# Second norm and router inside the attention across the batch, and modulation rows in the first layer's block

## What is computed

```python
mod = (silu(c) @ wmod).reshape(8, 6, 1, 256)
sa, ca, ga, sb, cb, gb = (mod[:, i] for i in range(6))
ga = (2 * (ga >= 0) - 1) * maximum(abs(ga), 0.25)      # gb likewise
x = x + ga * attention(layernorm(x) * (1 + ca) + sa)
x = x + gb * ffn(layernorm(x) * (1 + cb) + sb)
```

```python
h1 = hidden + attention_across_batch(layernorm(hidden) * w1 + b1)
tokens = layernorm(h1) * w2 + b2                       # the second norm
probs = softmax(tokens @ router_weight)                # 8 experts, top 2, capacity 1280
out = h1 + moe(tokens, probs)
```

## Time and profile before

| | us |
|---|---|
| median of 3 runs | 3240.66 |
| lowest, highest | 3238.57, 3241.61 |
| the profiled execution, its time | 3246.79 |
| the profiled execution, its span | 3245.0 |
| TensorE busy | 2931.1 (90%) |
| VectorE busy | 1657.6 (51%) |
| ScalarE busy | 1369.5 (42%) |
| GpSimd busy | 856.0 (26%) |
| mean granted TensorE clock | 0.944 |

### The profile page before, as it was taken

One profiled execution on the slowest core, in us unless ns is written; L12 is line 12 of the kernel. 1 busy time (PEld: TensorE's weight loads), 2 busy tenths in 40 slices (PEclk: granted clock), 3 DMA queues, 4 the chain that ended last, 5 costly groups with the idle time before them and its releaser, 6 DMA issues. The chain is left out here.

```text
span 3245.0 us, 52986 instructions
## 1 busy us (share of the span) xinstructions
PE 2931.1 (90%) x20772; PEld 1994.1 (61%) x20772; DVE 1657.6 (51%) x5057; ACT 1369.5 (42%) x2997; POOL 856.0 (26%) x830
## 2 busy tenths in 40 slices
PE   5889899975999999999999999999999688879993
PEld 2566666653575757666666666666565343668882
DVE  2566777644555544444444444455554576541114
ACT  2666666632444444445454535353433211112222
POOL 1001111122333332322323233233332100115554
PEclk8999999997999999999999999999999898669996
DMA  4110011004000000000000000100000000202325
GB/s 134 18 18 18 18 18 18 14 3 160 8 4 9 6 17 28 1 1 1 16 29 1 1 1 12 32 6 6 11 6 6 10 1 1 91 24 79 73 85 176
DMA packets 65135, 93.94 MB, mean 29 GB/s; under 512 B 9931, under 2 KB 52942, under 8 KB 63848
## 3 DMA queue, kind: packets, MB, share of 16 engines
q1 hardware_dynamic: 57208, 74.24, 7.9%
q0 software_dynamic: 7680, 16.32, 2.0%
HBM read 59.31 MB, written 27.36 MB: 27 GB/s over the span
## 5 line engine op out<-in xcount | busy, mean ns | idle before, releaser
L1371 PE MATMUL bank<-h2T,w 128*128 128x512 f32 x1024 | 479.4, 606 | 5.1 <-ACT gT L1309 3.7
L1409 PE MATMUL bank<-w,gT 128*128 128x256 f32 x2048 | 465.9, 381 | 0.0
L1409 PEld LDWEIGHTS bank<-w,gT 128*128 128x128 f32 x2048 | 379.3, 190 | 49.7 <-issue 0.5
L1046 POOL TENSOR_TENSOR prob<-prob,rsum 128x512 f32<-128x512 f32 (+1 forms) x256 | 238.1, 951 | 589.9 <-DVE rsum L1193 589.9
L1371 PEld LDWEIGHTS bank<-h2T,w 128*128 128x128 f32 x1024 | 182.4, 190 | 224.1 <-issue 173.9
L1309 ACT ACTIVATE gT<-bank,vec 128x512 f32<-128x512 f32 x256 | 175.1, 687 | 286.0 <-PE bank L1371 284.6
L633 ACT ACTIVATE y<-y,least 128x128 f32<-128x128 f32 (+3 forms) x512 | 251.9, 554 | 50.3 <-DVE least L520 50.2
L520 DVE CUSTOM_DVE_ANT_0 y<-bank,mask 128x128 f32<-128x128 f32 (+3 forms) x512 | 223.9, 486 | 77.0 <-PE bank L726 75.5
L1199 DVE COPY probT<-bank 128x1024 f32<-128x1024 f32 (+1 forms) x128 | 139.2, 1087 | 227.4 <-PE bank L1425 227.4
L1170 DVE CUSTOM_DVE_ANT_0 prob<-bank,mask 128x256 f32<-128x256 f32 (+1 forms) x512 | 164.3, 387 | 167.3 <-PE bank L1361 167.3
L1281 ACT ACTIVATE prob<-prob,least 128x256 f32<-128x256 f32 (+1 forms) x512 | 239.6, 471 | 15.8 <-DVE least L1170 15.4
(11 more groups left out here) (291 smaller groups left out, 5074.9 us busy)
## 6 DMA issues: line engine op xcount, KB each, us to landing
w<-in_W SPq DMA_DIRECT2D x8, 1024.0 KB, 5.5
expert_parts<-zeros SPq DMA_DIRECT2D x8, 1024.0 KB, 16.0
we<-in_we SPq DMA_DIRECT2D x16, 512.0 KB
rows<-modulation SPq DMA_DIRECT2D x40, 128.0 KB, 3.0
x<-in_x SPq DMA_DIRECT2D x8, 512.0 KB, 9.8
prob<-score SPq DMA_DIRECT2D x64, 64.0 KB, 2.4
probT<-score SPq DMA_DIRECT2D x64, 64.0 KB, 2.4
y<-expert_parts SPq DMA_DIRECT2D x8, 512.0 KB, 8.8
```

The lines of the kernel that those rows point to most:

```text
L1046: nc.gpsimd.tensor_tensor(two, two, rsum[:, at:at + 2].unsqueeze(2).to_broadcast([P, 2, width]), ALU.mult).then_inc(s["probs"], 1)
L1371: ins = nc.tensor.matmul(M[m % 2][:, :], w1[:, k, m * P:(m + 1) * P], h2T[:, k, :], start=(k == 0), stop=(k == KD - 1))
L1409: ins = nc.tensor.matmul(M[i][:, (t % 2) * D:(t % 2 + 1) * D], gT[:, m, t * P:(t + 1) * P], w2[:, m, :], start=(m == 0), stop=(m == MF - 1))
```

## The change

Two parts, independent of each other.

**The opening goes into the first layer's block.** `opening` is gone. The modulation becomes seven more pieces of the first layer's list: `("MOD", (l, m), 0)`, block m of layer l, and `("MT", i, 0)`, the turning of sa, ca (i = 0) or sb, cb (i = 1). `MOD (0, 0)` and `MT 0` stand first in `OPEN0`; the others go into parts 1 and 3 of slots 0 to 2. SyncE's order of loads is new: both cT, block (0, 0) of the weights, x of batch 0, the three projection matrices, x of batch 1, the other five blocks of weights; then `fixed` and the placements of batch 0; then x of batches 2 to 7, wo, the three ffn matrices and mu. Each has its own semaphore or count, and each user waits for its own. The six stores of the rows stand ahead of SyncE's part of slot 4, the wait for them ahead of slot 5. The weights and rows of the modulation lie in buffers that the layer uses later; `fixed` moves from y to probT. GpSimd makes the identity in place and its masks in another order.

```diff
+MODULATION = {(0, 1): [("MOD", (0, 1), 0)], (0, 3): [("MOD", (0, 2), 0)], (1, 1): [("MT", 1, 0)],
+              (1, 3): [("MOD", (1, 0), 0)], (2, 1): [("MOD", (1, 1), 0)], (2, 3): [("MOD", (1, 2), 0)]}
...
-OPEN0 = [("L", 0, 0), ("L", 1, 0), ("Q", 0, 0), ("Q", 1, 0), ("K", 0, 0), ("K", 1, 0), ("V", 0, 0), ("V", 1, 0),
+OPEN0 = [("MOD", (0, 0), 0), ("MT", 0, 0), ("L", 0, 0), ("L", 1, 0), ("Q", 0, 0), ("Q", 1, 0), ("K", 0, 0), ("K", 1, 0), ("V", 0, 0), ("V", 1, 0),
...
+                if n == QUADS:
+                    sp.wait_ge(s["mod_ready"], 6)
+                    for l in range(2):
+                        for m in range(3):
+                            sp.dma_start(c.mod_dram[l, :, m * T:(m + 1) * T], rows[l][m]).then_inc(s["store"], 16)
+                if n == QUADS + 1:
+                    sp.wait_ge(s["store"], 6 * 16)
...
+            def modulation(x):
+                _, (l, m), _ = x
+                full(dve, x)
+                block = rows[l][m]
+                emptied(nc.vector.tensor_copy(block, bank_of(x)[0:B, :]), x)
+                drained(dve, x)
+                if m == 0:
+                    v = block[:, D:2 * D]
+                    nc.vector.tensor_scalar(v, v, 1.0, None, ALU.add).then_inc(s["mod_ready"], 1)
+                    return
+                if m == 2:
+                    v = block[:, 0:D]
+                    nc.vector.tensor_scalar(v, v, 1.0, None, ALU.add)
+                v = block[:, 0:D] if m == 1 else block[:, D:2 * D]
+                steps(nc.vector.tensor_scalar(sign, v, 0.0, 2.0, ALU.is_ge, ALU.mult))
...
             stats(0)
+            taken(OPEN0[0:1])
             norm(0, None)
+            taken(OPEN0[1:2])
             stats(1)
...
+                    if kind == "MOD":
+                        l, m = i
+                        if l == 0 and m < 2:
+                            pe.wait_ge(s[("cond_loaded", "wm_loaded")[m]], (3, 5)[m] * 16)
+                        for k in range(KD):
+                            ins = nc.tensor.matmul(bank[0:B, :], cT[:, l, k, :], wm[l][m][:, k, :], start=(k == 0),
+                                                   stop=(k == KD - 1))
...
                         if i == 0 and kind == "Q":
-                            pe.wait_ge(s["load"], L + 9 * 16)
+                            pe.wait_ge(s["wqkv_loaded"], 3 * 16)
```

```diff
+def router_of(p):
+
+    return [("T2", (k, g), p) for g in range(2) for k in range(KD)], [("LG", 0, p)]
...
-    gaps[7] = [("AV", j, p) for j in (1, 0, 2)]
+    turned, logits = router_of(p - 1) if p else ([], [])
+    gaps[7] = [("AV", j, p) for j in (1, 0)] + turned + [("AV", 2, p)] + logits
...
+            by_place = c.token_rows.rearrange("(b t p) n -> t p b n", t=NT, p=P)
+            for p in range(NT):
+                sp.wait_ge(s["normed_rows"], p + 1)
+                sp.dma_start(by_place[p], rows2[:, :, :]).then_inc(s["rows_stored"], 16)
...
+            def router_stats(p):
+                for j in (2, 3):
+                    drained(dve, ("PROJ", j, p))
+                for i in range(B):
+                    ins = nc.vector.bn_stats(bn[:, i, :], c.y[:, i, p, :])
+                steps(ins)
+                for i in range(B):
+                    ins = nc.vector.bn_aggr(mv2[:, i, :], bn[:, i, :])
+                ins.then_inc(s["norm_stats"], 1)
+
+            def router_norm(p):
+                dve.wait_ge(s["norm_rstd"], p + 1)
+                if p:
+                    full(dve, ("T2", (KD - 1, 1), p - 1))
+                    dve.wait_ge(s["rows_stored"], 16 * p)
+                for i in range(B):
+                    ins = nc.vector.tensor_scalar(rows2[:, i, :], c.y[:, i, p, :], mv2[:, i, 0:1], rstd2[:, i:i + 1],
+                                                  ALU.subtract, ALU.mult)
+                ins.then_inc(s["normed_rows"], 1)
...
                 weighted(p)
+                if p:
+                    router_norm(p - 1)
                 if p + 2 < NT:
                     stats(p + 2)
...
                     added(p, j)
+                router_stats(p)
+            router_norm(LAST_TILE)
...
+                    if kind == "T2":
+                        k, g = i
+                        pe.wait_ge(s["normed_rows"], p + 1)
+                        for a in range(4):
+                            ins = nc.tensor.transpose(bank[:, a * P:(a + 1) * P],
+                                                      rows2[:, 4 * g + a, k * P:(k + 1) * P], c.ident[:, :])
+                    if kind == "LG":
+                        for k in range(KD):
+                            for g in range(2):
+                                drained(pe, ("T2", (k, g), p))
+                        for b in range(B):
+                            for k in range(KD):
+                                ins = nc.tensor.matmul(bank[:, b * E:(b + 1) * E], hT2[:, k, b * P:(b + 1) * P],
+                                                       c.wr[:, k, :], start=(k == 0), stop=(k == KD - 1))
```

More of the change, by code:

```diff
@@ L279, in work_of @@
                 (("L", 1, b + 2),))}[q]
-    parts = [[x for x in part if 0 <= x[2] < B] for part in LAST.get(n, mine)]
+    parts = [[x for x in part if 0 <= x[2] < B] + MODULATION.get((n, i), []) for i, part in enumerate(LAST.get(n, mine))]
     if 0 <= n - 1 < SLOTS:
@@ L570, in taken @@
                 for x in part:
+                    if x[0] == "MOD":
+                        modulation(x)
+                    if x[0] == "MT":
+                        mod_turned(x)
                     if x[0] == "OT":
@@ L763, in work @@
                     bank = bank_of(x)
+                    if kind == "MOD":
[5 more added lines that the diff above has]
+                                                   stop=(k == KD - 1))
+                    if kind == "MT":
+                        pe.wait_ge(s["mod_ready"], (1, 3)[i])
+                        for z, name in enumerate((("sa", "ca"), ("sb", "cb"))[i]):
+                            block, half = divmod(CHUNK[name], 2)
+                            for k in range(KD):
+                                first = D * half + k * P
+                                ins = nc.tensor.transpose(bank[:, (z * KD + k) * B:(z * KD + k + 1) * B],
+                                                          rows[0][block][:, first:first + P], c.ident[0:B, 0:B])
                     if kind == "L":
@@ L1555, in cross_pieces @@
             order += part
+    for part in router_of(LAST_TILE):
+        order += part
     return order
@@ L1815, in _ @@
                     taken(gaps[k])
+            for part in router_of(LAST_TILE):
+                taken(part)
         @block.tensor
@@ L1905, in _ @@
                 work(last)
+            for part in router_of(LAST_TILE):
+                work(part)
     c.loaded = loaded
@@ L1999, in _ @@
         def _(sp):
-            sp.dma_start(wr[:, :, :], d["wrouter"].rearrange("(k p) n -> p k n", p=P)).then_inc(s["moe_loaded"], 16)
-            sp.dma_start(gains[:, :], d["moe_ln"]).then_inc(s["moe_loaded"], 16)
             sp.dma_start(gate[:, :, :], mod_rows(c, 1, "gb")).then_inc(s["moe_loaded"], 16)
-            for b in range(B):
-                sp.wait_ge(s["normed_rows"], b + 1)
-                sp.dma_start(tokens(c.token_rows, b), rows(b)).then_inc(s["rows_stored"], 16)
             for e in range(E):
@@ L2355, in sb @@
             return st.enter_context(nc.sbuf_tensor(name, shape, dt))
-        def pair(first):
-            return [c.bank[:, first + i, :] for i in range(2)]
         c.x = sb("x", [P, B, NT, D])
```

377 lines of the change are left out of this document (135 added, 242 removed), and 3 rows, old and new, of the table SEMS.

## The result

| | before | after |
|---|---|---|
| time, median (lowest to highest) | 3241.14 us (3238.57 to 3246.97), 4 runs | 3209.81 us (3208.06 to 3210.66), 4 runs |
| profiled execution, span | 3246.79 us, 3245.0 us | 3208.06 us, 3206.3 us |
| first scores of layer 0 | 66.01 | 39.04 |
| first softmax across the batch | 2575.5 | 2543.8 |
| last addition to the router's maximum | 47.28 us | 20.82 us |

The time after is 0.990 of the time before (95% interval 0.9883 to 0.9917); a second set of five runs gave 3209.35 us and 0.9909 (0.9893 to 0.9925). The forecast was 3210.8.

What follows compares the result with a forecast made beforehand. TensorE runs at its higher level nearly throughout, except at the opening and the end of the attention across the batch, where it waits or runs low. -31.5 + 10.6 + 17.2 - 26.2 = -29.9 us, from 3240.66 to 3210.8; own range 3203 to 3219.

Steps and rivals of the forecast that it cites:

- Part A: Opening: fewer loads and one modulation block ahead bring first scores from 66.0 to 34.5, -31.5 us (bounds -33 and -27).
- the norm's 1.4: Opening: the first norm's four operations on VectorE take 1.4 us, making xn ready at 12.4.
- Part B: Slots 0 to 2 of the first layer: five modulation blocks and one turning add 10.6 us (bounds 5 and 17).
- rival 1: Inserted work falls into idle time: slots cost 5, tiles of the attention across the batch 11; 3199.0 us, chance 0.16.
- VectorE's chains: Slots 0 to 2: VectorE's copy of 0.7 per block, or 1.8 us of four operations for gates, delays next scores.
- Part C: Attention across the batch: statistics, turnings and router matmuls inserted in the tiles add 17.2 us (bounds 11 and 30).
- the low stretch: Tiles of the attention across the batch: one more stretch of TensorE at 1.2 GHz, 1.7 us lost.
- Part D: Tail, last addition to router's maximum: 21.0 us where 47.28 stood, -26.2, router matmuls priced at the low clock, 6.8.
- Rivals 2 and 4: Router matmuls lower the clock in the tiles: around its pieces, 3231, chance 0.13; or for all that follows, 3280, chance 0.03.
- rival 2: Clock low around router's pieces in three tiles: router 3.4, turnings 1.5, following projection 2 more; +20, 3231, chance 0.13.
- Rival 3: Opening stays bound by its loads or SyncE, front gains 6.7 less; 3217.5 us, chance 0.06.
- The signs: Next profile: first scores near 34.5, fifth slot and first tile's softmax 21 us earlier, 21 us from last addition to router's maximum.

Runs made afterwards that it cites:

- The first half alone: Kernel before with only the new opening and modulation pieces in the slots, second norm and router still in a separate stage; 3218.46 us, ratio 0.9931.
- experiment 5: Changed kernel with the router's TensorE pieces of tile 1 moved into tile 3's softmax, those of tile 2 behind tile 3's projections; 3193.05 us.
- experiment 7: Changed kernel with GpSimd's fixed work ahead of first rstd, router pieces of tiles 1 and 2 and tile 0's logits moved into tile 3; 3193.02 and 3191.12 us.

## Why the prediction was right

The time, 3209.81, is 1.0 us from the forecast, and the case was the forecast's own. Each of the four terms has the right sign, and those with bounds lie within them or at them. But three were off by 2 to 5.4 us, and that the sum came so close is luck. Step by step:

- **Part A** (-31.5): measured 66.01 - 39.04 = -27.0, at its upper bound. The loads and the first block came as worked out (silu at 6.41, from a piece taken at 5.8, and 5.72 to 7.11 in the other profiles; the block's copy at 10.34), though the listed terms add up to 12.7 without any wait, not to 12.4. The term that failed is "the norm's 1.4": it measured 6.54. GpSimd's fixed rows were costed as "ready at about 14" for SyncE's sake only; that they run beside the norm was not asked, although held such a case (5.10 for eight steps instead of 2.66). The projections began 5.7 us later than forecast (21.00 for 15.3). The stretch from there to the scores, which was to stay 19.25, took 18.04, as its 16 matmuls ran in 8.73 instead of 9.96, and gave 1.2 back. With GpSimd out of the way the scores start at 34.15, as forecast (34.5). That SyncE's moved loads cost nothing fits: the wait ahead of the first scores is 4.52, as before.
- **Part B** (+10.6): against the second profile of the kernel before, +5.2 in slots 0 to 3 (5.8 and 5.9 by two further profiles); doubling the matmuls costs 8.2 there and 10 in the time. They grew by 3.0, 0.2 and 2.0, not by 4.3, 2.6 and 3.7. The size was less by 5.4 and came to the lower bound, 5, which is also rival 1's figure. The step that failed is the cover: "block one adds 1.8", "one block without a gate 1.9 + little" and "two: 3.7" gave each block its own time, while TensorE's idle time took 3.1 of the 8.3 us. The other 2.3 were to come from VectorE's chains; no slot grew by more than TensorE's own added work, so these chains (9.25 us more in all) added nothing of their own, though no run takes them out alone. A second set found that idle time used up and cost 8.2.
- **A + B**: the two misses, +4.5 and -5.4, cancel. The first half alone gave -20.7 for -20.9; that it was so close is luck.
- **Part C** (+17.2): tiles 1, 2 and 3 are longer by 6.0, 5.4 and 7.8, +19.2. The pieces were as priced or less (3.0 for the turnings and 3.5 from the router's first matmul to the projections, for 3.4 and 3.4), and the idle 2.37 ahead of the next scores did take its part, as the prediction had it: TensorE no longer waits there. The term that was mis-sized is the low stretch, counted once with 1.7. It came behind the router's matmuls in each of the three tiles: the projections took 5.39 for 3.62 in tiles 1 and 2 and 8.58 for 7.07 in tile 3, together some 5 us. In tile 2 1.7 came back, for the low stretch of 2731 to 2737 was gone. For tile 1 the terms close: 3.0 + 3.5 + 1.8 - 2.4 = 5.9 of the 6.0 measured. The prediction's own sign for being wrong in part C, a grant of 0.5 behind the router's matmuls while the projections run, is there (0.51 from 2645.80 to 2649.20): by it this step was wrong, though the size stayed within its bounds.
- **Part D** (-26.2): 20.8 us for 21.0, and the router's matmuls 6.97 for 6.8. Pricing them at the lower level was right: TensorE waits 9.14 us for the norm and was granted 0.50 while it worked behind it. The Trainium skill's rule in "TensorE: Matmul & The Clock Gate", Part 1, that sustained work releases the throttle, was given 3.4 us here; the trace disagrees with applying it to this stretch. In experiment 5 TensorE works up to 2771.7 and has hardly a wait behind it; the tail was granted 0.75, its last 32 router matmuls 0.81, and they took 4.43: that is the direction of the rule.
- **Rival 1** (3199.0) was right for part B and wrong for part C (19.2, where it had 11). Its time would have needed both, and the opening at -31.5.
- **Rivals 2 and 4** would have shown in the tiles: tiles 1 and 2 were granted 0.92 and 0.91 in both profiles of the changed kernel, and 0.94 and 0.91 before. The clock fell for part of one projection block per tile, not for the tile. Of rival 2's three terms one came, "the following projection 2 more" (1.8, 1.8 and 1.5); the router's matmuls and the turnings themselves ran at the high level in tiles 1 and 2.
- **Rival 3** did not happen: silu started at 6.41, under the 8 that was set for it.
- **The signs**: the fifth slot came 24.8 us earlier than in the first profile of the kernel before and 21.6 earlier than in the second (21 was said), the first softmax 21.0 earlier than in the second.
- The comparison with the profile before needs care: the two spans differ by 38.7 us, the medians by 31.3. The prediction had put its profile 6.1 above the median and taken that off; the second profile (3236.17, slots 3 to 5 without the low clock) supports it. With that one the terms add up: -26.8 for the scores' start (65.83 to 39.04), 5.2 for slots 0 to 3, 0.6 for the rest of the layers up to the first softmax, 19.2 and -26.5 are -28.3, and the spans differ by 28.1.

## What to carry to other kernels

Idle time of an engine takes inserted work only where it stands in that engine's order ahead of a wait that it does not set itself: the same router matmuls cost their time ahead of the projections, and 1.5 to 1.8 us more because what followed ran at the lower level, and nothing behind the projections, where TensorE waited for VectorE anyway. Of every constant that GpSimd writes, ask what VectorE does at that moment; here moving five instructions ahead of the first norm's power gave 4 to 5 us. When two profiles differ by more than the medians, compare stage by stage with the granted clock beside the lengths, and take a second profile of the kernel before.

## What the runs showed of the hardware

- VectorE's norm steps stood still while GpSimd worked: 1.94 us (median) for a step beside the iota, copy and memset of 1.85, 1.99 and 1.90, instead of 0.35 (1.38 for four). Each such step lasts about as long as one GpSimd instruction. The Trainium skill ("SBUF — State Buffer", "SBUF: two separate sides") describes this as a port pair of the two engines that one holds for its whole instruction while the other waits; the trace agrees, with these durations, though no run here tells which instructions take part.
- The same 32 router matmuls (128 rows by 8 columns) took 3.63, 3.89, 4.43, 4.54, 4.78 and 6.97 us in different places, and 64 of them 11.31. A gap on TensorE should be sized by the upper figure.
- TensorE's level fell behind these matmuls although it had no idle time: busy for 3.59 of 3.59 us at 1.00, then 0.51 for the next 3.4 us, under the projections. Without them, with the turnings still there, the same projections took 3.62 us instead of 5.39 (experiment 7). The kernel before shows the same from the other side: busy for 39.64 of 40 us with turnings and such matmuls, and granted 0.50 throughout.
- The executions of the kernel before lie in two groups, 3233 to 3242 and 3246 to 3248 us, 15 of 50 in the upper one. One profile each showed low clock in slots 3 to 5 at 3246.79 and none there at 3236.17; what decides between them was not found.
